# The transpose of a unit's probabilities as one DMA transfer or as two, in a two-layer cross-attention kernel

## What is computed

```python
x = x + xattn0(layernorm(x), ctx, mask, q_w, q_b, k_w, k_b, v_w, v_b)      # masked softmax, 16 heads x 32
x = x + ffn0(layernorm(x), packed_weight, weight_scale, bias)              # rows quantised to int8 steps, ternary weights
x = x + xattn1(layernorm(x), ctx, Wq, bq, Wk, bk, Wv, bv, Wo, bo)          # softmax, 16 heads x 64
x = x + ffn1(layernorm(x), w_freq_real, w_freq_imag, bias)                 # FFT, sparse complex product, inverse FFT
```

## Time and profile before

| | us |
|---|---|
| median of 3 runs | 1131.73 (1128.67 to 1133.52) |
| the profiled execution's own time | 1130.68 |
| its span, first to last instruction | 1128.9 |
| PE busy in matmuls | 922.6 (82%) |
| DVE busy | 811.0 (72%) |
| ACT busy | 670.1 (59%) |
| POOL busy | 566.4 (50%) |
| the hardware DMA queue's packets, as a share of 16 engines' span | 55.5% |

### The profile page before, as it was taken

The page is one execution under the profiler, slowest core; times in us unless marked ns, Lnnn a source line. Parts: engine busy times, 40 slices in busy tenths (PEclk is TensorE's granted clock), DMA queues, the critical chain, the costliest instruction groups (busy, mean ns, idle before and its releaser), DMA issues.

```text
span 1128.9 us, 18053 instructions
## 1 busy us (share of the span) xinstructions
PE 922.6 (82%) x6227; PEld 505.6 (45%) x6227; DVE 811.0 (72%) x1417; ACT 670.1 (59%) x1936; POOL 566.4 (50%) x602
## 2 busy tenths in 40 slices
PE   0488976766866998999799789989997996798794
PEld 0345763333423554555455445544554554444441
DVE  6487766457869778978886897789777868725632
ACT  2236773247558677767885776778667757415601
POOL 2303662605247366746764584668466745804504
PEclk9789989787878999999999999999998999799798
DMA  9461484456656656584766757555847555521602
GB/s 282 99 159 26 97 161 85 98 107 148 151 82 114 136 89 109 108 186 84 134 139 136 114 110 176 101 108 108 186 79 127 126 105 97 111 79 33 117 38 74
DMA packets 352474, 130.40 MB, mean 116 GB/s; under 512 B 333439, under 2 KB 342592, under 8 KB 349439
## 3 DMA queue, kind: packets, MB, share of 16 engines
q1 hardware_dynamic: 352383, 129.25, 55.5%
HBM read 33.57 MB, written 15.96 MB: 44 GB/s over the span
## 4 chain that ended last, share of the span: by engine, by line
PE 47%; DVE 17%; ACT 10%; issue 10%; DMA 7%; POOL 6%; SPq 3%; POOLq 0%; ACTq 0%; DVEq 0%
PE wb L188 13%; PE wb L190 13%; PE wb L189 13%; ACT pr L933 5%; PE wb L1470 3%; DMA prT<-ph 3%; DVE xh L1195 2%; SPq L568 2%; DMA xT<-xh 2%; DVE parts L1013 2%; ACT xh L958 2%; DVE ph L1277 2%; POOL xr L795 1%; PE scores L188 1%; POOL pr L769 1%
## 5 line engine op out<-in xcount | busy, mean ns | idle before, releaser
L769 POOL TENSOR_TENSOR pr<-pr,sm 128x616 f32<-128x616 f32 x128 | 174.2, 1361 | 231.6 <-DVE sm L1272 216.2
L933 ACT ACTIVATE pr<-scores,bound,factor 128x77 f32<-128x77 f32 x640 | 255.6, 419 | 8.6 <-ACT bound L927 0.8
L188 PE MATMUL wb<-xT,wq_hl 128*128 128x512 f16 (+1 forms) x400 | 155.7, 389 | 27.8 <-DMA xT<-xh 20.3
L189 PE MATMUL wb<-xT,wq_hl 128*128 128x512 f16 (+1 forms) x400 | 155.4, 389 | 0.0
L190 PE MATMUL wb<-xT,wq_hl 128*128 128x512 f16 (+1 forms) x400 | 155.0, 387 | 0.0
L946 ACT ACTIVATE ph<-pr 128x618 f16<-128x618 f32 x128 | 93.3, 730 | 80.3 <-POOL pr L769 50.8
L933 ACT ACTIVATION_READ_ACCUMULATOR pr<-scores,bound,factor 128x1 f32 x640 | 132.7, 207 | 0.0
L188 PE MATMUL wb<-wo_hl,qc 128*128 128x512 f16 x276 | 105.6, 382 | 8.7 <-DVE x L1211 4.6
L189 PE MATMUL wb<-wo_hl,qc 128*128 128x512 f16 x276 | 105.5, 382 | 0.0
L190 PE MATMUL wb<-wo_hl,qc 128*128 128x512 f16 x276 | 105.4, 382 | 0.0
L1211 DVE SCALAR_TENSOR_TENSOR xr<-wb,factor,xr 128x512 f32<-128x512 f32 x72 | 52.2, 736 | 57.9 <-PE wb L190 57.9
(11 more groups left out here) (212 smaller groups left out, 2443.2 us busy)
## 6 DMA issues: line engine op xcount, KB each, us to landing
xr<-in_x SPq DMA_DIRECT2D x6, 1024.0 KB, 5.9
out_x<-xr SPq DMA_DIRECT2D x6, 1024.0 KB, 5.1
xr<-in_wk SPq DMA_DIRECT2D x3, 1024.0 KB, 6.7
xr<-in_wq SPq DMA_DIRECT2D x3, 1024.0 KB, 10.2
xr<-in_wv SPq DMA_DIRECT2D x3, 1024.0 KB, 6.8
k1b<-scr_k SPq DMA_DIRECT2D x16, 154.0 KB, 5.3
scr_k<-k1b SPq DMA_DIRECT2D x7, 308.0 KB, 7.2
x<-in_x SPq DMA_DIRECT2D x2, 1024.0 KB, 7.1
```

The source lines that it names most:

```text
L188: pe.matmul(out, lhs(0), rhs(0), start=start, stop=False, **kw)
L189: pe.matmul(out, lhs(0), rhs(1), start=False, stop=False, **kw)
L769: pool.tensor_tensor(v, v, s, ALU.mult).then_inc(probs_ready, 1)
L933: ins = act.activation(pr[U % 3][:, h // 4, cols], sc[:, U % 2, h // 4, cols], ACT.Exp, bias=bound[:, U % 2, h:h + 1], scale=k["factor"][: ...
```

## The change

The transfer of a unit is replaced by two, of 6 blocks each: the high half behind a wait on `probs_hi`, and the low half behind the wait on the low half's writer. Each raises `turned[u]` by 16, so the three places that wait for it count to 32 a unit. The wait that the transpose's target is free stays ahead of both transfers, and now comes behind the wait on the high half rather than behind the wait on the low half.

```diff
@@ turn (SP)
-                sp.wait_ge(*probs_lo(U))
+                sp.wait_ge(probs_hi, U + 1)
                 reader = ("Y", "pv", 4 * half + 3, b - 2) if stage == "X" else ("X", "pv", t, b + 1)
                 if reader in FILL:
                     sp.wait_ge(bank_full, FILL[reader] + 1)
                 elif stage == "X" and b == 0 and u >= 2:
                     sp.wait_ge(lo_done, split_count("WF"))
-                sp.dma_start_transpose(prT[:, t, half, :, :, :, :].rearrange("p h g c n -> p (h g c) n"),
-                                       ph[:, U % 2, :, :, :, :].rearrange("p h g c n -> p (h g c n)")).then_inc(turned[u], 16)
+                for h in range(2):
+                    if h == 1:
+                        sp.wait_ge(*probs_lo(U))
+                    sp.dma_start_transpose(prT[:, t, half, h, :, :, :].rearrange("p g c n -> p (g c) n"),
+                                           ph[:, U % 2, h, :, :, :].rearrange("p g c n -> p (g c n)")).then_inc(turned[u], 16)
@@ probs_high (ACT)
-                    act.wait_ge(turned[before[1]], 16 * (PASS[before] + 1))
+                    act.wait_ge(turned[before[1]], 32 * (PASS[before] + 1))
@@ values0 (PE)
-                    pe.wait_ge(turned[u], 16 * (PASS["X", u, b] + 1))
+                    pe.wait_ge(turned[u], 32 * (PASS["X", u, b] + 1))
@@ values1 (PE)
-                        pe.wait_ge(turned[u], 16 * (PASS["Y", u, b] + 1))
+                        pe.wait_ge(turned[u], 32 * (PASS["Y", u, b] + 1))
```

## The result

The change makes the kernel slower by 0.6%: 1138.07 us median (1137.31 to 1141.58, 6 runs) against 1131.57 us for before in the same comparison (1128.67 to 1136.98, 6 runs), a ratio of 1.0063 with a 95% interval of 1.0034 to 1.0092. The profiled execution took 1141.58 us (span 1139.6), 3.5 us above the median, so its rows show somewhat more than the typical loss; before's was near its median.

The account below looks back on a forecast made before the run. PE held 47% of the chain of waits, the turn's transfer 3%. Terms -0.5 - 1.0 - 0.6 + 0.8 + 1.5 = +0.2 us on 1130.68 gave 1130.9 us, no change, range 1125.5 to 1136.5 us.

Parts of the forecast that it names:

- item 5: Five turns on the chain queued behind another transpose on SP: +0.3 us each (0 to 0.8), +1.5 us in all.
- The fifth late turn: One of five chain turns behind another transpose on SP, (Y, 0) at 640.34: +0.3 us.
- The price of a half turn: 6 blocks issue in 1.13 us and land in 2.8 us, so a turn sent ahead lands 0.85 us sooner.
- item 2: Turn at 1053.29, gap between halves 1.57 us, longer than the issue: 3.81 - 2.8, so -1.0 us.
- Items 1 to 3: Chain places released by the low half's writer: turns at 984.46 (-0.5 us) and 1053.29 (-1.0), issues at 107.97 and 261.49 (-0.6).
- item 3: Issues at 107.97 and 261.49, each 1.13 us in place of 1.48 and 1.40: -0.6 us.
- Item 4: Issue at 263.90 behind another transfer on SP, two issues in place of one of 1.50 us: +0.8 us.
- Steady waits at `values1`: In five batches PE starts 0.85 us sooner at line 1470 but gains nothing, as the wait moves to DVE.
- Rival B: Faster: eight waits, mostly PE's steady ones, keep 0.85 us each because DVE's queue is released sooner; 1124.1 us, chance 0.10.
- ACT's waits: Six waits of about 5 us at line 946 behind the value loads grow some 0.8 us, covered by later idle time.
- rival A: Slower: SP's queue becomes the wait; late turns pay fully, 2.5 us, and places behind value loads 4.8; 1138.2 us, chance 0.12.
- Rival C: High half doesn't go ahead: a turn's two issues queue up whatever SP's idleness; 1133.0 us, chance 0.04.

Follow-up runs that it names:

- x7_only: Kernel before with only the turn of stage X's last unit (X, 7) made as two transfers; 1139.55 us, ratio 1.0032; again on another chip 1140.15 us, 1.0055.
- all_but_x7: Changed kernel with the turn of (X, 7) alone whole again, the other units in two transfers; 1134.07 us, ratio 0.999 to before.
- x34_only: Kernel before with only the turns of (X, 3) and (X, 4), behind the value loads and the batch's load, in two transfers; 1134.78 us, ratio 0.9994.
- y01_only: Kernel before with only the turns of (Y, 0) and (Y, 1), behind two row transposes, in two transfers; 1133.95 us, ratio 0.9994.
- whole_late: Changed kernel with the five units SP reaches late, (X, 3), (X, 4), (X, 7), (Y, 0), (Y, 1), whole again; 1137.2 us, ratio 1.001 to before.
- no_early: Changed kernel with both transfers of every unit issued behind the wait on the low half, none ahead; 1147.28 us, ratio 1.0141 to before.
- before_rows: Kernel before, whole turns, with the transpose of rows (3, 0) issued behind the turn of (X, 7); 1122.91 us, ratio 0.9918; again 1122.05 us, 0.9895.

## Why the prediction was wrong, point by point

**The step that failed is item 5 of the sum**, the turns behind another transpose, which I sized at +0.3 us each, +1.5 us in all and +1.2 us for the four of them that are turns of (X, 7). The turn of (X, 7) alone cost 0.32 and 0.55% (x7_only twice), 4 to 6 us. The place and the direction were right and the size was not.

- The landing was priced well: 4.0 us forecast for the pair alone and +0.3 us a turn; the four turns on the chain took 4.13, 4.60, 4.62 and 4.12 us in place of 3.72, 4.30, 4.35 and 4.18, 0.2 us more on average. The low half landed in 2.83 to 2.85 us each time; the high half's issue took 1.70 and 1.72 us at two of them and 1.23 and 1.24 at the others.
- PE's wait was not: at the same four places it grew by 0.84, 0.42, 0.39 and 0.79 us. I had taken the later landing, counted from SP's issue, for the whole cost. At 948.64 the turn landed no later after its issue, but the row transpose ahead of it took 2.76 us to issue, 1.92 before.
- The count: I took the chain's four such turns as the places that matter. Off the chain, near 628, PE's wait there had been for DVE (2.01 us); it became a wait of 2.44 us for the turn. Every batch has this place, and 1.2 us became about 3 us of added waiting at `values0`.
- The rest, 1 to 3 us, stays open, and so does the share of the clock in it. From the product near 422 to the same one near 941, five batches on, before took 519.3 us, the changed kernel 526.4, x7_only 526.6 and 526.0, all_but_x7 520.8. But all of PE's waits in that stretch sum to 41.9, 40.8, 42.5, 42.9 and 41.3 us: what was added at `values0` was mostly taken off later waits, and the stretch took longer outside the waits. In the pair with the extra matmuls it is the other way round: 518.4 and 522.0 us, with waits of 29.1 and 32.6 us, so there the waits are all of it. These are single executions (x34_only, which lost nothing over its runs, took 524.6 us), and no run separates the two shares in the kernel without extra matmuls.
- The fifth late turn of the earlier trace rows, (Y, 0) at 640.34, which I priced like the others, cost nothing (y01_only).

**The price of a half turn**: the landing was right, 2.8 us forecast and measured. The issue took 1.25 us, not 1.13, just outside my bound of 1.23. By the Trainium skill, "DMA: Bandwidth & Descriptors", section "Anatomy of one DMA", a transfer takes about 2 us and its bytes at 436 GB/s, which the page gives for transfers issued by GpSimd; SP issues these. By that figure the saving would be an estimate of 0.45 us. The trace doesn't agree with it: item 2's 3.81 us became 2.74 us.

**Items 1 to 3**: PE's waits fell by 0.4 us (3.04 to 2.65) and 1.3 us (3.09 to 1.78), forecast 0.5 and 1.0; item 3's issue near 262 took 1.21 us in place of 1.40. Yet the kernels that split only or mostly turns which SP awaits gained nothing that shows (whole_late 1.001, all_but_x7 0.999), so the 2.1 us that these items took off can't be confirmed. **Item 4**: two issues of 1.26 and 1.29 us in place of 1.50, +1.1 us, forecast +0.8.

**Steady waits at `values1`**: over five batches PE's waits for the turn there fell from 7.3 to 3.1 us and those for DVE's line 1204 rose from 3.1 to 6.4. Most of the gain was handed on. Rival B, which kept it, is out: 1124.1 us would be a ratio of 0.994, and all_but_x7 and whole_late have 0.9962 and 0.9986 as their lower ends.

**ACT's waits** for the turn went from 29.5 to 33.9 us, the longest from 5.2 to 6.6: between the 5 to 6 us forecast and the 8 us of rival A.

**Rival A** gave the right time, 1138.2 us, by luck. It put two thirds of its price on the value loads, and x34_only shows none there. Its other third, late turns that pay in full, is nearest to what happened, but at one unit only, and that unit alone cost what A had for all five late turns (0.8 us each, 4.0 us) or more. The Trainium skill's rule named with it ("DMA: Bandwidth & Descriptors", section "Rules for kernel authors", many small transfers joined into one large) agrees with these runs where the second issue comes on top: no_early lost 1.4%. It doesn't show in whole_late, which lost nothing that can be seen. **Rival C** is out: SP issued the high halves ahead.

## What to carry to other kernels

Cutting a transfer in two can pay only where the issuing engine is idle when the first piece is ready and the reader has nothing else to wait for behind it; in this kernel it paid nowhere (0.999 and 1.001 without the costly turn). Where the issuing queue comes late, both pieces are ready and the second issue is pure delay, so list for each waited-for transfer what stood ahead of it in that queue. And look there first: moving one transfer that nobody needed yet from ahead of the waited-for one was worth more (0.8 to 1.0%) than any way of cutting it that was tried. A wait that the reader has in every batch should be counted in every batch, also where another wait hides it on the chain.

## What the runs showed of the hardware that was not expected

The granted clock dropped to 1.2 GHz for part of the stretch behind a cluster of PE waits (1.43 and 3.22 us within 14 us), and by a single pair of profiles all of the difference could be put down to it. Extra matmuls in the waits held it at 2.4 GHz through the middle of the run and gained each kernel 0.3 to 0.4%; with the new order they didn't hold it (0.98) and gained nothing. Below 8 blocks a transpose's issue doesn't shrink: 1.44 us for 12 blocks, 1.23 for 8, and 1.25 for 6. What stays open is why before_rows gained 9 to 12 us, when PE's waits for that turn had been 1.0 to 1.6 us a batch: the waits for xT went with it, but no run was made to tell which part of the new order does that.
